# Gather of one edge group and scatter of an older one, interleaved tile by tile on TensorE

## The reference

```python
# L0: five times
h = leaky(x @ W1[l] + b1[l]) @ W2[l] + b2[l]                    # per node
e = leaky(edge_attr_32 @ We1[l] + be1[l]) @ We2[l] + be2[l]     # per edge
agg = segment_sum(h[src] * e * dot_scale[l], dst, 3125)
x = layernorm(x + agg * res_w[l]) * ln_g[l] + ln_b[l]
# L1: rst = segment_sum((x * deg_out**-0.5 @ weight)[src], dst) * deg_in**-0.5 + bias
# L2: two attention convolutions over the edges
# L3: x + segment_sum(relu(x[src] + edge_attr_64), dst)
```

## Time and profile before

| | |
|---|---|
| median of 3 runs | 7844.31 us (7841.6 to 7846.52) |
| profiled execution | 7817.12 us, its span 7815.2 us |
| TensorE matmul busy | 6285.5 us, 80% |
| weight load busy | 5013.5 us, 64% |
| VectorE busy | 5308.1 us, 68% |
| ScalarE busy | 2933.7 us, 38% |
| GpSimd busy | 2771.1 us, 35% |
| mean granted TensorE clock | 0.853 |

### The profile page before, as it was taken

The page is one execution under the profiler, slowest core; times in us unless marked ns, Lnnn a source line. Parts: engine busy times, 40 slices in busy tenths (PEclk is TensorE's granted clock), DMA queues, the critical chain, the costliest instruction groups (busy, mean ns, idle before and its releaser), DMA issues. The chain is left out here.

```text
span 7815.2 us, 276543 instructions
## 1 busy us (share of the span) xinstructions
PE 6285.5 (80%) x87510; PEld 5013.5 (64%) x87511; DVE 5308.1 (68%) x15345; ACT 2933.7 (38%) x5054; POOL 2771.1 (35%) x4280
## 2 busy tenths in 40 slices
PE   4888888846666588788788788788789998999887
PEld 3666666634444377677677677677776776777676
DVE  7555554579999777677677677677865554555677
ACT  2444444424444433333333333233653332333333
POOL 2666666643333144344344344344000000000343
PEclk9888888865555699899899899799768998999999
DMA  2666666622222577577577577577441111111576
GB/s 78 172 180 181 182 179 177 182 72 73 71 73 71 187 191 191 140 193 196 138 196 193 139 193 196 133 194 192 158 178 51 68 60 44 68 60 60 138 202 174
DMA packets 1403296, 1098.82 MB, mean 141 GB/s; under 512 B 1012406, under 2 KB 1171821, under 8 KB 1393467
## 3 DMA queue, kind: packets, MB, share of 16 engines
q1 hardware_dynamic: 887994, 797.65, 33.3%
q0 software_dynamic: 224768, 240.90, 12.7%
q10 hardware_dynamic: 290304, 57.05, 4.0%
HBM read 815.28 MB, written 278.78 MB: 140 GB/s over the span
## 5 line engine op out<-in xcount | busy, mean ns | idle before, releaser
L544 POOL DMA_DIRECT2D big<-rows x2592 | 1415.2, 546 | 3721.9 <-issue 2284.6
L1309 PE MATMUL ps<-big 128*128 128x64 bf16 x20736 | 1292.7, 198 | 377.7 <-issue 356.3
L1296 PE MATMUL ps<-big 128*128 128x64 bf16 x41472 | 1418.2, 196 | 100.2 <-DVE big L1783 57.5
L1296 PEld LDWEIGHTS ps<-big 128*128 128x128 fp8e4 x41472 | 1338.4, 100 | 175.4 <-issue 135.5
L1309 PEld LDWEIGHTS ps<-big 128*128 128x128 bf16 x20736 | 985.7, 99 | 643.9 <-issue 431.1
L814 POOL DMA_INDIRECT rows<-big x800 | 1022.9, 1279 | 606.3 <-issue 360.9
L1018 ACT CAST big<-big 128x512 bf16<-128x512 f32 x720 | 445.1, 618 | 1293.4 <-DVE big L1796 1230.4
L1796 DVE TENSOR_TENSOR big<-ps,big 128x512 f32<-128x512 f32 x720 | 497.8, 691 | 608.3 <-PE ps L1296 594.1
L1255 PE MATMUL ps<-identb,big 128*128 128x128 bf16 x2304 | 472.6, 308 | 359.9 <-DVE big L1684 353.6
L1573 DVE SCALAR_TENSOR_TENSOR big<-big 128x1000 f32<-128x1000 f32 (+1 forms) x300 | 359.5, 1198 | 579.1 <-ACT big L905 435.5
L1212 PEld LDWEIGHTS ps<-big 128*125 128x125 f32 (+1 forms) x4800 | 682.6, 212 | 101.5 <-issue 57.6
(11 more groups left out here) (263 smaller groups left out, 9350.4 us busy)
## 6 DMA issues: line engine op xcount, KB each, us to landing
big<-ohsD SPq DMA_DIRECT2D x432, 512.0 KB, 3.7
big<-ohdD SPq DMA_DIRECT2D x432, 320.0 KB, 4.1
big<-rows POOLq DMA_DIRECT2D x2592, 32.0 KB, 3.6
big<-rows SPq DMA_DIRECT2D x2592, 32.0 KB, 3.5
big<-maskD SPq DMA_DIRECT2D x50, 1600.0 KB, 6.7
big<-rows ACTq DMA_DIRECT2D x1728, 32.0 KB, 3.3
big<-keyT SPq DMA_DIRECT2D x100, 488.3 KB
maskD<-big SPq DMA_DIRECT2D x25, 1600.0 KB, 6.2
```

Source lines behind the costliest of these rows:

```text
L544: eng.dma_start(edge[:, s.r, j, :], rows[bass.ds(v[s.r * (hi - lo) + j - lo], P), col]).then_inc(landed[s.r], 16)
L1296: last = pe.matmul(pG[g.r][:, j * D:(j + 1) * D], ohsR[:, g.r, at:at + P].bitcast(F8), slices[:, g.r, q // QUAD, (3 * k + c) * D:(3 * k + ...
L1309: last = pe.matmul(pacc[:, bass.ds(w[j], D)], hot[:, g.r, j * P:(j + 1) * P], parts[:, g.r, c, j * D:(j + 1) * D], start=False, stop=False ...
```

## The change

On TensorE the functions `scatter` and `gather`, called one after the other in a step, become `turn_over`. It waits for all that both need, first for the scatter and then for the gather, and then goes over the eight tiles: the six gather matmuls of tile j of the newer group, then the three scatter matmuls of tile j of the older one. The semaphores `gathered` and `scattered` both rise with the last matmul of their kind, that is both at the end of the step. Both kinds of pass call it. The order of the matmuls within the gather, and within the scatter, stays the same, and so does what each of them computes.

```diff
-            def gather(s, base, nth):
+            def gather_ready(g, base, nth):
+                pe.wait_ge(ohs_loaded[g.r // 2], (nth * TRIPS + g.t) * 16 + 16)
+                pe.wait_ge(sliced, base + g.i + 1)
+                if not g.known or g.i >= RING:
+                    pe.wait_ge(m_ready, base + g.lag(RING).i + 1)
+                hold(pe)
+
+            def gather(g, j):
+                q = j // QUAD
+                for k in range(2):
+                    at = ((q * 2 + k) * QUAD + j % QUAD) * P
+                    for c in range(3):
+                        last = pe.matmul(pG[g.r][:, j * D:(j + 1) * D], ohsR[:, g.r, at:at + P].bitcast(F8),
+                                         slices[:, g.r, q, (3 * k + c) * D:(3 * k + c + 1) * D],
+                                         start=(k + c == 0), stop=(k + c == 3))
+                return last
+
+            def scatter_ready(g, base, nth):
+                pe.wait_ge(lo_ready, base + g.i + 1)
+                pe.wait_ge(hot_made, base + g.i + 1)
+                pe.wait_ge(hot_loaded[g.r // 2], (nth * TRIPS + g.t) * 16 + 16)
+
+            def scatter(g, j, w):
+                for c in range(3):
+                    last = pe.matmul(pacc[:, bass.ds(w[j], D)], hot[:, g.r, j * P:(j + 1) * P], parts[:, g.r, c, j * D:(j + 1) * D],
+                                     start=False, stop=False, skip_group_check=True)
+                return last
+
+            def turn_over(s, w, base, nth):
+
+                to, of = s.lag(S_LAG), s.lag(G_LAG)
+                if s.live(S_LAG):
+                    scatter_ready(to, base, nth)
                 if s.live(G_LAG):
-                    g = s.lag(G_LAG)
...
+                    gather_ready(of, base, nth)
+                for j in range(GT):
+                    if s.live(G_LAG):
+                        got = gather(of, j)
+                    if s.live(S_LAG):
+                        put = scatter(to, j, w)
+                if s.live(G_LAG):
+                    got.then_inc(gathered, 1)
                 if s.live(S_LAG):
...
+                    put.then_inc(scattered, 1)
@@ both passes
-                    scatter(s, two[s.r % 2], l * NG, l)
-                    gather(s, l * NG, l)
+                    turn_over(s, two[s.r % 2], l * NG, l)
```

More of the change, by code:

```diff
@@ L1281, in open_sums @@
                     pe.matmul(bank(b), zerob[:, :], zerob[:, 0:1].to_broadcast([P, 512]), start=True, stop=False, skip_group_check=True)
-            def gather(s, base, nth):
-                if s.live(G_LAG):
-                    g = s.lag(G_LAG)
[L1286 to L1299, removed]
@@ L1301, in scatter @@
-            def scatter(s, w, base, nth):
-                if s.live(S_LAG):
[L1303 to L1311, removed]
+            def gather_ready(g, base, nth):
[4 more added lines that the diff above has]
+                hold(pe)
@@ L1356, in body @@
                         two[:] = blocks(PE, s.i)
-                    scatter(s, two[s.r % 2], base, nth)
-                    gather(s, base, nth)
+                    turn_over(s, two[s.r % 2], base, nth)
                 steps(pe, body)
```

## The result

The changed kernel takes **7423.32 us** (median; 7419.31 to 7432.07) against 7845.42 us before (7841.6 to 7849.61): a ratio of 0.9463, with a 95% interval of 0.9447 to 0.948. Forecast were 7543 us in a range of 7440 to 7770. The profiled execution took 7420.97 us, its span 7419.4.

A forecast was written before the change was run, and what follows sets the result against it. TensorE's own sequencer was taken as the bound, at 3.474 us a layer step, with SyncE next at 3.03. Gains of 700 x 0.354 + 140 x 0.38 = 301 us from the median 7844.31 gave 7543 us, range 7440 to 7770.

The forecast's parts named there:

- the dear dispatch: TensorE's sequencer: 12 more instructions a tile at 9.3 ns each, 0.296 us a tile, 3.53 us a step, no gain left.
- rival a: TensorE's sequencer stays the bound, tiles at 0.29 us or more: 7620 to 7844 us; chance 0.14.
- The full queue in the gather: TensorE's sequencer runs 0.47 us, 16 weight-and-matmul pairs, ahead in a gather, idle because its queue is full.
- The 2.78 us of TensorE alone: TensorE's step in the changed kernel: 2.09 us of array work plus 0.69 us of mean losses.
- SyncE's floor: SyncE's issues in layer passes: four steps need 12.11 us, 3.03 us a step, whatever TensorE does.
- blocks that do not fit: Layer passes: SyncE's 6.74 and 5.37 us blocks against uneven TensorE steps add an estimated 0.09 us, giving 3.12 a step.
- the allowance of 0.18 us a step: Last pass: three engines stand at 2.77 or 2.78 us a step, and 2.95 was taken.
- a floor of 7455: Whole kernel at the floors themselves: 700 x 0.444 + 140 x 0.56 = 389 us gained, 7455 us.
- (b): One-hot loads become the bound; landing 2 us longer gives 3.3 us a step, 7720 us; chance 0.10.
- (c): TensorE's alternating weight types and PSUM banks cost 0.164 us a change back, 4.09 us a step, 8384 us; chance 0.08.
- (d): TensorE's clock falls, 0.048 us a matmul, 4.15 us a step, 8435 us; chance 0.03.
- (e): Nothing changes: gaps, not matmuls, set TensorE's pace, 3.47 us a step; chance 0.03.

The follow-up runs named there:

- e6: Changed kernel with ScalarE's edge issues ahead of its cast and edge tiles shared 2, 3, 3 between SyncE, GpSimd and ScalarE: 7335.08 us, ratio 0.9378.
- e3: Kernel before, with every scatter tile at a fixed column instead of a register address; the table load fell away too: 7371.6 us, ratio 0.9383.
- e7: Kernel before, with only each scatter's first tile at its register address, the other seven at fixed columns, table load kept: 7369.0 us, ratio 0.943.
- e8: Changed kernel, with only each scatter's first tile at its register address and the other seven at fixed columns: 7385.2 us, ratio 0.9433.
- e10: Changed kernel with three gather tiles ahead of the table load and scatter's waits, the last three scatter tiles alone: 7383.39 us, ratio 0.943.
- e5: Changed kernel with ScalarE's two edge issues of a step ahead of its cast of the message, shares unchanged: 7416.31 us, ratio 0.9475.
- e1: Changed kernel with a group's eight edge tiles shared 2, 3, 3 between SyncE, GpSimd and ScalarE instead of 3, 3, 2: 7528.37 us, ratio 0.9602.
- e4: Changed kernel with joined waits at the step's head but matmuls not mixed, whole scatter then whole gather: 7958.65 us, ratio 1.0143.
- e11: Changed kernel with ScalarE's edge issues ahead of its cast, shares 2, 3, 3, and the gather three tiles ahead: 7312.41 us, ratio 0.9364.

## Why the prediction was wrong

**Right.** TensorE's step: 2.30 us from first start to last end in a step without the load, as written, and 0.26 us a tile. The array's pace and not the dear dispatch holds (rival a is out: with 0.296 us a tile eight would take 2.37; measured are 2.12 us from first to last start, to which 0.03 for one matmul is to be added). The full queue in the gather was the right sign of a sequencer with time to spare. The 2.78 us of TensorE alone agree with the 11.1 us a turn, 2.77 a step, estimated above. The next bound in the layers: SyncE, with 12.09 us for four steps against 12.11 forecast; e6 took it away, and e3, e7, e8 and e10 all came down to it (12.07 to 12.08) and no further. The scattered semaphore at the step's end cost nothing that shows: SyncE issues with no wait in most blocks.

**Wrong: the size, in the step from SyncE's floor to the pass.** I had 3.03 us a step, added 0.09 for blocks that do not fit, and took 140 steps at 3.12 and eight at the old 3.474, 464.6 us for a layer pass. Measured are 445.8. SyncE issues for 144 groups, 36 times 12.11 us or 436 us, and the steps of filling and emptying add not their old price but, in e10, 6 us. So two terms were mis-sized. The floor of a pass came out at 452 us (140 x 3.03 + 8 x 3.474) where e10 shows 441, 11 us too much. The allowance for blocks that do not fit was 0.09 us a step or 12.6 us a pass, where the changed kernel stands 5 us over that floor, 8 us too much; its four-step periods are 12.2 to 12.3 us in the mean, a wait of some 0.03 to 0.05 us a step. Five passes of 18.8 us are 94 us. In the last pass 140 x 2.95 + 8 x 3.33 = 440 us stood against 428.3, 11 us more. These 105 us are the whole difference of the passes (406 less 301). In the last pass the allowance of 0.18 us a step was about right (428 less 36 x 11.08 = 399 and 6 for filling leaves 23 us, 0.16 a step); there the eight steps at their old price are the error. The remaining 16 of the 422 us are not in the passes: the profiled execution of before, from which I worked, was 28 us under the median, that of the changed kernel 2 us, and outside the passes the span grew by 10 us.

**The range** was wrong for the same reason. Its low end of 7440 lay just below a floor of 7455, and that floor was itself wrong, for it counted 140 of 148 steps at SyncE's pace and eight at the old one. Counted on whole passes, 36 x 12.11 and 36 x 11.08 us, it is 5 x 436 + 399 = 2579 us, 485 below the old sum. So 7360 us should have been the low end of the range, by an estimate that leaves out filling and emptying.

**The rivals.** (b) did not come as a bound: ohdD lands after 4.4 us, not 5.4, and TensorE's idle time put down to it is 9 us in 350 of the second layer. But the nearest thing to it was missed: ScalarE's edge issues, which serve a message only two steps later. They cost the changed kernel 6 to 9 us in the last pass (e5) and, as e6 shows, all that e1 lost. (c) did not come: 16 changes of weight type and banks in a step leave the matmuls 0.029 us apart, from bf16 back to fp8 as well. (d) did not come: the granted clock rose from 0.97 or less to 0.99, with 16 changes of banks a step. The Trainium skill (TensorE: Matmul & The Clock Gate, "A second HAM failure mode: psum-queue depth-cycling") says of a kernel with matmuls of 512 columns that cycling through PSUM banks made the engine idle briefly and its clock swing; in this kernel, with 64 columns, the measurement decides, and the clock stays at 0.99. (e) did not come.

**e4** shows an error that the forecast did not need: the losses of four steps were put at 2.75 us with joined waits, where those of before add up to 3.35, a gain of 0.15 us a step. Alone the joining loses 1.4%. In the mix the lead at a step's end pays for it.

## What to carry to other kernels

Where matmuls with addresses from registers are slower than the same matmuls with fixed ones, look for a phase in which the sequencer stands behind a full queue, and mix the two finely; joining only their waits may lose. Before forecasting a gain on one engine, add up the issue time of each DMA queue over a loop turn, and multiply it by the groups that it issues for, not by the steps of the pipeline, to get the floor of a pass. Where an engine's gaps repeat from turn to turn and its waiting instructions follow at once on the work before them, as in e11, it waits for nobody, whatever the row names as releaser. And when an issue is moved to another engine, ask how far ahead of its use that engine issues: here the move helped only once the issues stood ahead of the work that waits.

## What the runs showed of the hardware

In the kernel before, 17 matmuls of a gather had still to start when TensorE's sequencer passed its end, in all 340 gathers of the six passes where the trace lets one count: 0.475 us of lead at the array's full pace (294 of them) and 0.886 us at its slower pace (46). Register work of eight addresses cost a scatter of 24 matmuls 0.67 us where nothing covered it (1.54 against 0.87 us), and nothing within a step where 0.26 us of matmuls a tile did. Alternating fp8 and bf16 weights, and PSUM banks, every three to six matmuls of 64 columns cost nothing: in the changed kernel the median distance of starts is 0.029 us across either change. With an output at a fixed address, and no other reader, the load of the address table vanished from the program, so that e3 removed two things; e7 was needed to part them. One edge issue of SyncE took 0.57 us of its queue in the layers (3.42 / 6) and 0.50 in the last pass (3.00 / 6), and 0.34 us of that is the issuing instruction; the rest is register work.
